# First layer of a four-layer image kernel: its matmuls cut into 32x32 tiles, its weighting by w2 and sum over branches moved to TensorE

## The chip, the cores and the metric

The kernel runs on 1 core of one Trainium2 chip. The metric is the device time of one execution in microseconds (us); lower is better. Five engines work at once, each with its own queue of instructions: TensorE (PE: matmuls, with their weight loads shown apart as PEld), VectorE (DVE), ScalarE (ACT), GpSimd (POOL) and SyncE (SP: it issues the DMAs). They wait for one another by semaphores.

## What is computed

x holds 8 images of 128 x 128 pixels with 32 channels. Four layers follow, each on a normalised x and each added to x. The change touches the first alone:

```python
def _gn(v, G=32, eps=1e-05):          # per image and channel over all pixels
    ...
def _L0_conv_ref(x, w1, wg, w2):      # w1, w2: (32, 4); wg: (4, 32, 32)
    y = _gelu(x[..., :, None] * w1)
    z = _gelu(jnp.einsum('bhwim,moi->bhwmo', y, wg))
    out = jnp.einsum('bhwmc,cm->bhwc', z, w2)
    return out
...
x = x + _L0_conv_ref(_gn(x), L0_conv_w1, L0_conv_wg, L0_conv_w2)
x = x + _L1_conv_ref(_gn(x), L1_conv_kernel)
x = x + _L2_conv_ref(_gn(x), ...)
x = x + _L3_conv_ref(_gn(x), ...)
```

So the first layer has four branches m. In each, every channel is scaled by w1[:, m] and goes through gelu (y), a 32x32 matrix wg[m] mixes the channels, a second gelu gives z, and the output is the sum of w2[:, m] * z over the four branches. All of it is float32.

## The kernel before

The 8 images are worked in two slabs of 4 (s = 0, 1). A slab's 4 images x 32 channels fill the 128 partitions (partition = 32 * image + channel), and its 16,384 pixels lie along the free dimension of the SBUF tile X. A slab goes through 8 stages (0: load and transpose, 1: the first layer, 2: the second, 3 and 4: the third, 5 to 7: the fourth); all engines meet between stages (stage_end). After both slabs comes a last part that scales and stores.

Stage 1 takes the slab in 8 chunks of 2048 pixels (CHUNK), each with 4 branches, so a slab has 32 units k = 4 * i + m. A unit is:

- gelu_y (L547, ACT): y = gelu(scale * X chunk + bias), 128 x 2048, into yb[m]; the normalisation and w1 are folded into scale and bias (l0s).
- the matmuls of L333 (PE): 4 matmuls of 128 x 512 with wg[m], which is stored as a block-diagonal 128 x 128 matrix with wg[m] once per image, into 4 of the 8 PSUM banks. Even branches take banks 0 to 3, odd ones 4 to 7, so PE can project one unit while ACT reads the other.
- gelu_z (L554, ACT): gelu of the 4 banks into zb[m % 2].
- L698 (DVE): acc = zb * w2[:, m] + acc, 128 x 2048; the last of the four writes X.

ACT's order is gelu_y(k + 2), gelu_z(k), gelu_y(k + 3), gelu_z(k + 1) and so on: the y of two units ahead lies between two z. Only at the slab's end are there z with no y between them (the last three). PE's L330 waits for y of unit k (s_y) and for the bank set to be free (s_zs, slot(k): z of unit k - 2 has been read). gelu_z waits for the projection (s_zp) and for a free zb (s_x1). The semaphores made by rsem are rings: slot(k) lets work k start when work k - ring is done, after(k) waits for work k itself. After each chunk DVE measures X with four bn_stats (L704), after the last it aggregates them (L676), POOL works out the next layer's coefficients (L953 to L956), and stage 2 begins.

Stages named below: stage 3 has matmuls 32 columns wide (L410: output partitions C * g, all 128 rows), stage 4 has matmuls of 32 rows by 64 columns (L448, function r_sum: 8 combinations of row group and column half) and transposes (L459); ACT copies the results of L448 (L614). The last part has, again and again, 4 transposes (L515) and a matmul of 512 columns (L253).

Of the kernel before, what the change touches and what calls it, by code (L numbers as in the profile page):

```python
# [24 lines left out]
G = P // C  # L25
# [42 lines left out]
def build(nc, x, consts, choose, out):  # L68
# [5 lines left out]
    with ctx:  # L74
# [19 lines left out]
        bns = sb("bns", 16)  # L94
        ps = ctx.enter_context(nc.psum_tensor("ps", [P, 8, BANK], fp32))
# [10 lines left out]
        wg = c("wg").rearrange("p (m n) -> p m n", m=MULTI)  # L106
        wq = c("wq").rearrange("p (h n) -> p h n", h=HEADS)
# [24 lines left out]
        zb, _e = part(_e, [RING, CHUNK])  # L132
        acc, _ = part(_e, [CHUNK])
# [55 lines left out]
        s_zs = rsem("z_ready", "act")  # L189
        s_x1 = rsem("z_added", "dve")  # L190
# [117 lines left out]
        def _(pe):  # L308
# [3 lines left out]
            for s in range(NS):  # L312
# [14 lines left out]
                with pe.Fori(0, PIX // CHUNK) as i:  # L327
                    for m in range(MULTI):
                        k = s * UNITS + i * MULTI + m
                        pe.wait_ge(s_y, k + 1)  # L330
                        pe.wait_ge(s_zs, slot(k))
                        for b in range(4):
                            last = pe.matmul(ps[:, 4 * (m % 2) + b, :], wg[:, m, :], yb[:, m, b * BANK:(b + 1) * BANK],  # L333
                                             start=True, stop=True)
                        last.then_inc(s_zp, 1)
# [192 lines left out]
        def _(act):  # L528
# [5 lines left out]
            for s in range(NS):  # L534
# [131 lines left out]
        def _(dve):  # L666
            start_rings(dve, "dve")
            for s in range(NS):
# [430 lines left out]
```

## Time and profile before

| | us |
|---|---|
| median of 3 runs | 1118.27 (1116.99 to 1118.3) |
| the profiled execution, its own time | 1117.37 |
| its span, first to last instruction | 1115.4 |
| busy PE / DVE / ACT / POOL | 888.9 / 845.1 / 600.1 / 324.9 |
| stage 1, first slab, first gelu_y to first coefficient | 130.4 (41.09 to 171.51) |
| stage 1, second slab | 129.9 (520.01 to 649.91) |

The time of an execution is 1.97 us over its span. The two runs of stage 1 are 23% of the span. A busy time is the union of an engine's instructions: overlapping ones are counted once, so "busy" is no measure of how much work goes through. The granted clock of PE has two levels, 1.2 GHz (0.50 in the profile) and 2.4 GHz (1.00). Each float32 matmul of the code stands in the trace as two MATMUL records, each with a weight load of its own: the 4 matmuls x 64 units of L333 are 256 in the code and 512 in the trace. The start of a group of instructions, its length, its engine, its line and its tiles are one row of the timeline; "idle before" is how long that engine had stood still and who released it.

### The profile page before, as it was taken

The numbers are of one execution on the slowest core, as the hardware profiler recorded it, in microseconds if no ns is written. First come the engines' busy times: TensorE is split into PE (matmuls) and PEld (weight loads), VectorE is DVE, ScalarE is ACT, GpSimd is POOL, SyncE is SP. The second block draws the span as 40 slices with busy tenths as digits, with TensorE's granted clock in tenths as the row PEclk, the third lists the DMA queues.
The fourth block names the chain that finished last, engine by engine and source line by source line (L and its number), as shares of the span: only waits on it lengthen the run. The fifth ranks groups of instructions, "written<-read, shape, count | busy, mean of one in ns | idle before, by whom it ended". The sixth has DMA issues, their size and how long they took to land. (4 is left out here: it accounts for less than half of the span.)

```text
span 1115.4 us, 21429 instructions
## 1 busy us (share of the span) xinstructions
PE 888.9 (80%) x6876; PEld 591.1 (53%) x6876; DVE 845.1 (76%) x1207; ACT 600.1 (54%) x695; POOL 324.9 (29%) x265
## 2 busy tenths in 40 slices
PE   5699986979997667965999949799966588676774
PEld 4343336978875465343433349788854563233332
DVE  7577787987868844885778879877778446799796
ACT  5899982323333153546999923233332444466564
POOL 0000008500009910510000067000089304465564
PEclk8899997989998678988999969999986688899897
DMA  9100000000000020242000000000000200033334
GB/s 304 36 1 0 0 0 1 0 1 1 0 1 2 1 75 3 72 139 88 0 0 0 0 1 1 1 1 0 1 2 2 75 0 1 0 114 113 113 113 151
DMA packets 51305, 39.40 MB, mean 35 GB/s; under 512 B 1600, under 2 KB 50880, under 8 KB 51008
## 3 DMA queue, kind: packets, MB, share of 16 engines
q1 hardware_dynamic: 51264, 38.85, 11.0%
q8 instruction: 25, 0.41, 0.1%
q14 instruction: 16, 0.13, 0.0%
HBM read 22.07 MB, written 16.78 MB: 35 GB/s over the span
## 5 line engine op out<-in xcount | busy, mean ns | idle before, releaser
L333 PE MATMUL ps<-work,cst 128*128 128x512 f32 x512 | 235.9, 608 | 17.3 <-ACT work L547 13.5
L333 PEld LDWEIGHTS ps<-work,cst 128*128 128x128 f32 x512 | 94.3, 193 | 157.6 <-issue 143.4
L547 ACT ACTIVATE work<-X,l0s 128x2048 f32 (+1 forms) x64 | 136.7, 2141 | 3.8 <-SPq L291 3.8
L253 PE MATMUL ps<-ST,work 128*128 128x512 f32 (+1 forms) x256 | 131.7, 638 | 7.5 <-DVE work L866 5.4
L554 ACT ACTIVATE work<-ps 128x2048 f32<-128x2048 f32 x64 | 123.1, 1924 | 7.1 <-PE ps L333 6.8
L988 POOL TENSOR_TENSOR work<-cst,ksum 128x512 f32<-128x512 f32 x64 | 69.5, 1105 | 174.5 <-SPq L291 172.6
L778 DVE TENSOR_TENSOR work<-ps,cst 64x512 f32<-64x512 f32 x128 | 88.1, 688 | 37.8 <-PE ps L400 36.0
L953 POOL TENSOR_TENSOR co<-mv,cst 128x1 f32<-128x1 f32 x8 | 1.5, 189 | 383.0 <-DVEq L243 296.7
L576 ACT ACTIVATE work<-ps 128x512 f32<-128x512 f32 x80 | 47.8, 597 | 99.6 <-PE ps L353 99.6
L1023 POOL TENSOR_TENSOR work<-X,work 128x512 f32<-128x512 f32 x64 | 82.1, 1286 | 58.9 <-DVE work L913 58.9
L364 PE MATMUL ps<-cst,work 128*128 128x143 f32 x640 | 96.5, 296 | 1.4 <-DVE X L728 1.2
L698 DVE SCALAR_TENSOR_TENSOR work<-work,cst 128x2048 f32<-128x2048 f32 x32 | 75.2, 2351 | 24.5 <-ACT work L554 24.3
L913 DVE SCALAR_TENSOR_TENSOR work<-work 128x512 f32<-128x512 f32 x64 | 92.1, 1444 | 0.0
L364 PEld LDWEIGHTS ps<-cst,work 128*128 128x128 f32 x640 | 86.3, 196 | 5.0 <-DVE X L728 3.3
L640 ACT ACTIVATE work<-work,bns 128x512 f32<-128x512 f32 x64 | 52.0, 813 | 58.7 <-DVE work L908 58.7
L585 ACT ACTIVATE work<-ps 128x512 f32<-128x512 f32 x64 | 38.2, 597 | 83.7 <-PE ps L400 83.7
L476 PE MATMUL ps<-cst,work 128*128 128x96 f32 x512 | 62.2, 288 | 23.1 <-ACT work L623 23.1
L623 ACT ACTIVATE work<-X,co 128x512 f32 x64 | 51.4, 812 | 51.7 <-POOLq L243 44.4
L459 PE MATMUL ps<-cst,work 128*128 128x128 f32 x256 | 52.4, 352 | 32.5 <-DVE X L820 32.4
L1007 POOL TENSOR_TENSOR work<-work 128x512 f32<-128x512 f32 x32 | 40.6, 1270 | 124.4 <-ACT work L635 124.4
L515 PE MATMUL ps<-cst,work 128*128 128x128 f32 x256 | 45.7, 305 | 39.0 <-POOL work L1023 38.8
L515 PEld LDWEIGHTS ps<-cst,work 128*128 128x128 f32 x256 | 29.2, 150 | 87.0 <-POOL work L1023 87.0
(96 smaller groups left out, 1649.3 us busy)
## 6 DMA issues: line engine op xcount, KB each, us to landing
work<-x SPq DMA_DIRECT2D x32, 512.0 KB, 4.6
out<-work SPq DMA_DIRECT2D x64, 256.0 KB, 2.8
work<-choose SPq DMA_DIRECT2D x2, 2048.0 KB, 7.9
cst<-consts SPq DMA_DIRECT2D x1, 1009.5 KB, 9.0
cst<-consts SPq DMA_DIRECT2D x1, 64.0 KB, 1.9
```

The lines of the kernel that those rows point to most:

```text
L253: return nc.tensor.matmul(ps[:, bank, :], sel[:, n, :], ST[:, ds(s * (4 * H), 4 * H)], start=True, stop=True)
L333: last = pe.matmul(ps[:, 4 * (m % 2) + b, :], wg[:, m, :], yb[:, m, b * BANK:(b + 1) * BANK], start=True, stop=True)
L364: last = pe.matmul(ps[:, DEEP + 2 * (q % 2) + par, at:at + OW * OH], patch[:, q, k, :], c("fir"), start=True, stop=True)
L476: last = pe.matmul(ps[:, u, w * COLS:w * COLS + COLS], xc[:, u, w * H:w * H + H], c("w9"), start=True, stop=True)
L515: last = pe.transpose(ps[:, DEEP + n % DEEP, w * P:w * P + P], row[:, n % ROWS, w * H:w * H + H], ident)
L547: act.activation(yb[:, m, :], X[:, ds(s * PIX + i * CHUNK, CHUNK)], ACT.Gelu, scale=l0s[:, m:m + 1], bias=l0s[:, MULTI + m:MULTI + m + 1]) ...
L554: act.activation(zb[:, m % 2, :], ps[:, 4 * (m % 2):4 * (m % 2) + 4, :].rearrange("p a b -> p (a b)"), ACT.Gelu).then_inc(s_zs, 1)
L698: dve.scalar_tensor_tensor(acc if m < MULTI - 1 else x_in, zb[:, m % 2, :], c("w2")[:, m:m + 1], acc if m else x_in, ALU.mult, ALU.add).th ...
L778: last = dve.tensor_tensor(o, k_in, bias, ALU.add)
L913: dve.scalar_tensor_tensor(row[:, u, :], row[:, u, :], LEAKY, row[:, u, :], ALU.mult, ALU.max).then_inc(s_fl, 1)
L988: pool.tensor_tensor(qb[:, hf, :, :, :], c("bq").rearrange("p (j o i) -> p j o i", o=1, i=WS).broadcast_to([P, WS, half, WS]), ksum[:, ds( ...
L1023: pool.tensor_tensor(rows4(row[:, u, :]), columns(s, n), rows4(row[:, u, :]), ALU.add).then_inc(s_fo, 1)
```

## The change

The projection is cut into 16 matmuls per unit. Tile (g, k4) takes image g's 32 partitions of yb (rows 32g to 32g + 31), piece k4 of 512 pixels, and the 32x32 block of wg[m]; it writes to PSUM bank g, partitions 32 * k4 to 32 * k4 + 31. The four banks 0 to 3 then hold z with the pieces along the partitions and the images along the banks. gelu_z reads these four banks in every unit (before: two sets of four in turn), so the projection of unit k + 1 waits for gelu_z(k).

The weighting and sum are 16 more matmuls per unit (weigh_z). Each has 32 rows (piece k4) and 32 columns (image g), its weights are diag[rows, m, :], a 32x32 diagonal matrix of w2[:, m], and it adds to bank 4 + k4, partitions 32g onwards, from the first branch (start) to the last (stop). Banks 4 to 7 so hold the sum over the branches in X's own layout, and DVE adds them to X once per chunk. weigh_z of a chunk's first branch waits until DVE has read the chunk before. zb and acc shrink to zb alone; w2d is a new tile of 128 columns, filled by four POOL instructions at the start.

PE's program for stage 1 is no longer a loop: it is written out for the 32 units, in the order projection of unit k + 1, then weigh_z of unit k.

```diff
-                with pe.Fori(0, PIX // CHUNK) as i:
+                def project_y(i, m):
+
+                    k = s * UNITS + i * MULTI + m
+                    pe.wait_ge(s_y, k + 1)
+                    pe.wait_ge(s_zs, slot(k))
+                    for k4 in range(4):
+                        for g in range(G):
+                            rows = slice(C * g, C * g + C)
+                            last = pe.matmul(ps[C * k4:C * k4 + C, g, :], wg[rows, m, C * g:C * g + C],
+                                             yb[rows, m, k4 * BANK:(k4 + 1) * BANK], start=True, stop=True)
+                    last.then_inc(s_zp, 1)
+
+                def weigh_z(i, m):
+
+                    k = s * UNITS + i * MULTI + m
+                    pe.wait_ge(s_zs, after(k, 1))
+                    if m == 0:
+                        pe.wait_ge(s_x1, slot(i + s * (PIX // CHUNK)))
+                    for g in range(G):
+                        for k4 in range(4):
+                            rows = slice(C * k4, C * k4 + C)
+                            last = pe.matmul(ps[C * g:C * g + C, 4 + k4, :], diag[rows, m, :], zb[rows, m % 2, g, :],
+                                             start=(m == 0), stop=(m == MULTI - 1))
+                    last.then_inc(s_ws, 1)
+
+                pe.wait_ge(s_diag, 1)
+                project_y(0, 0)
+                for i in range(PIX // CHUNK - 1):
                     for m in range(MULTI):
-                        k = s * UNITS + i * MULTI + m
-                        pe.wait_ge(s_y, k + 1)
-                        pe.wait_ge(s_zs, slot(k))
-                        for b in range(4):
-                            last = pe.matmul(ps[:, 4 * (m % 2) + b, :], wg[:, m, :], yb[:, m, b * BANK:(b + 1) * BANK],
-                                             start=True, stop=True)
-                        last.then_inc(s_zp, 1)
+                        project_y(i + (m + 1) // MULTI, (m + 1) % MULTI)
+                        weigh_z(i, m)
...
                 def gelu_z(i, m):
                     k = s * UNITS + i * MULTI + m
                     act.wait_ge(s_zp, k + 1)
-                    act.wait_ge(s_x1, slot(k))
-                    act.activation(zb[:, m % 2, :], ps[:, 4 * (m % 2):4 * (m % 2) + 4, :].rearrange("p a b -> p (a b)"),
-                                   ACT.Gelu).then_inc(s_zs, 1)
+                    act.wait_ge(s_ws, slot(k))
+                    act.activation(zb[:, m % 2, :, :], ps[:, 0:4, :], ACT.Gelu).then_inc(s_zs, 1)
...
                 with dve.Fori(0, PIX // CHUNK) as i:
+                    n = i + s * (PIX // CHUNK)
                     x_in = X[:, ds(s * PIX + i * CHUNK, CHUNK)]
-                    for m in range(MULTI):
-                        k = s * UNITS + i * MULTI + m
-
-                        dve.wait_ge(s_zs, after(k))
-                        dve.wait_ge(s_x1, slot(k) + 1)
-                        dve.scalar_tensor_tensor(acc if m < MULTI - 1 else x_in, zb[:, m % 2, :],
-                                                 c("w2")[:, m:m + 1], acc if m else x_in, ALU.mult, ALU.add
-                                                 ).then_inc(s_x1, 1)
+                    dve.wait_ge(s_ws, after(i * MULTI + (s * UNITS + MULTI - 1)))
+                    dve.scalar_tensor_tensor(x_in, ps[:, 4:8, :].rearrange("p a b -> p (a b)"), 1.0, x_in,
+                                             ALU.mult, ALU.add).then_inc(s_x1, 1)
```

On TensorE, at the start of stage 1, the row of the program before (one loop body, run 8 times; "x4" are four matmuls in a row):

```order
L327 UNCONDITIONAL_BRANCH
L327 ISA
L333 MATMUL ps<-work,cst 128x512 x4
L330 REGISTER_ALU
L333 MATMUL ps<-work,cst 128x512 x4
L330 REGISTER_ALU
L333 MATMUL ps<-work,cst 128x512 x4
```

and of the changed program, where L338 is the projection and L351 the weighting:

```order
L338 MATMUL ps<-work,cst 32x512 x32
L351 MATMUL ps<-work,w2d 32x512 x16
L338 MATMUL ps<-work,cst 32x512 x16
L351 MATMUL ps<-work,w2d 32x512 x16
L338 MATMUL ps<-work,cst 32x512 x16
L351 MATMUL ps<-work,w2d 32x512 x16
```

The first two projections stand together, then weighting and projection take turns, and each projection stands ahead of the weighting of the unit before it.

On VectorE, in the same stage, before:

```order
L697 REGISTER_ALU [waits z_ready]
L698 ISA [waits z_added]
L698 SCALAR_TENSOR_TENSOR work<-work,cst,X 128x2048
L696 REGISTER_ALU
L698 SCALAR_TENSOR_TENSOR work<-work,cst 128x2048 [waits z_added,z_ready]
L696 REGISTER_ALU
L698 SCALAR_TENSOR_TENSOR work<-work,cst 128x2048 [waits z_added,z_ready]
```

and of the changed program:

```order
L719 UNCONDITIONAL_BRANCH [waits stage_ended]
L719 ISA
L723 ISA [waits z_weighted_and_summed]
L723 SCALAR_TENSOR_TENSOR X<-ps,X 128x2048
L725 REGISTER_ALU
L728 ISA [waits chunk_added]
```

Four instructions per chunk have become one, which waits for PE where the four waited for ACT. The order on ScalarE is as it was; gelu_z now waits for z_weighted_and_summed where it waited for z_added.

## Rows read from the trace of the kernel before

**Rows 1.** Steady stage 1: length, busy PE, PEld, DVE, ACT, POOL; PEclk.
```profile
99.39:155.55 56.16, 55.04 (x121) 21.59 (x120) 43.34 (x30) 56.16 (x32) 0.00 (x0) 1.00 0.00 0
```

**Rows 2.** L333: ns min/median/max; L554: busy us, mean ns | idle before, releaser.
```profile
L333 PE MATMUL ps<-work,cst x512: 592/592/1222, 43.2 to 641.1; 128*128 128x512 f32 x171
...
L554 ACT ACTIVATE work<-ps 128x2048 f32<-128x2048 f32 x64 | 123.1, 1924 | 7.1 <-PE ps L333 6.8
```

**Rows 3.** Timeline of the steady part: start us, length us, engine, line.
```profile
101.37 1.93 ACT L554 ACTIVATE work<-ps 128x2048 f32<-128x2048 f32 x1
...
103.42 0.30 PEld L333 LDWEIGHTS ps<-work,cst 128*128 128x128 f32 x2 [0.87 <-issue]
103.95 0.19 PEld L333 LDWEIGHTS ps<-work,cst 128*128 128x128 f32 x1 [0.24 <-issue]
104.38 0.19 PEld L333 LDWEIGHTS ps<-work,cst 128*128 128x128 f32 x1 [0.24 <-issue]
...
105.12 1.93 ACT L554 ACTIVATE work<-ps 128x2048 f32<-128x2048 f32 x1
```

**Rows 4.** Timeline, start of stage 1, first slab, then second.
```profile
41.09 6.06 ACT L547 ACTIVATE work<-X,l0s 128x2048 f32<-128x2048 f32 x3 [1.19 <-SPq L291]
43.24 23.41 PE L333 MATMUL ps<-work,cst 128*128 128x512 f32 x49 [6.75 <-ACT work L547]
48.97 1.88 ACT L554 ACTIVATE work<-ps 128x2048 f32<-128x2048 f32 x1 [1.82 <-PE ps L333]
...
527.37 1.88 ACT L554 ACTIVATE work<-ps 128x2048 f32<-128x2048 f32 x1 [1.29 <-PE ps L333]
```

**Rows 5.** Timeline, end of stage 1, first slab.
```profile
157.51 3.98 ACT L554 ACTIVATE work<-ps 128x2048 f32<-128x2048 f32 x2
...
163.36 1.88 ACT L554 ACTIVATE work<-ps 128x2048 f32<-128x2048 f32 x1 [1.87 <-PE ps L333]
165.27 2.35 DVE L698 SCALAR_TENSOR_TENSOR X<-work,cst 128x2048 f32 x1 [0.93 <-ACT work L554]
```

**Rows 6.** Timeline, groups of small tiles in stages 3 and 4.
```profile
260.02 1.08 PE L410 MATMUL ps<-work 128*32 128x128 f32 x32
...
335.56 1.26 PE L448 MATMUL ps<-work,cst 32*64 32x128 f32 x64 [2.05 <-ACT work L614]
...
336.88 1.94 ACT L614 ACTIVATE work<-ps 128x1024 f32<-128x1024 f32 x2 [1.37 <-PE ps L448]
...
365.84 2.01 PE L448 MATMUL ps<-work,cst 32*64 32x128 f32 x64
```

**Rows 7.** Inside the L448 group at 335.56: weight loads, then matmuls in flight.
```profile
335.56:335.67 0.11, 0.11 (x16) 1.00 0.00 0
...
335.80:335.81 0.01, 0.01 (x16) 1.00 0.00 0
```

**Rows 8.** PE busy, granted clock: last part, stage 4, stage 1's start.
```profile
990.00:1020.00 30.00, 22.31 (x89) 1.00 0.46 140
372.00:390.00 18.00, 10.95 (x101) 0.59 0.00 1
...
47.00:48.00 1.00, 1.00 (x4) 0.85 0.00 0
```

**Rows 9.** Timeline of PE: last part, then stage 4.
```profile
983.39 0.66 PE L515 MATMUL ps<-cst,work 128*128 128x128 f32 x4 [0.56 <-POOL work L1023]
983.88 1.02 PE L253 MATMUL ps<-ST,work 128*128 x2
...
378.91 2.24 PE L459 MATMUL ps<-cst,work 128*128 128x128 f32 x8 [2.03 <-DVE X L820]
```

**Rows 10.** VectorE reading PSUM; the page's instruction fetches; POOL after loading.
```profile
L908 DVE SCALAR_TENSOR_TENSOR work<-X,vall,ps 128x512 f32<-128x512 f32 x64 | 47.1, 735 | 7.7 <-PE ps L253 7.6
...
q8 instruction: 25, 0.41, 0.1%
...
38.86 0.19 POOL L953 TENSOR_TENSOR co<-mv,cst 128x1 f32<-128x1 f32 x1 [25.42 <-DVE mv L676]
```

More of the change, by code:

```diff
@@ L94, in build @@
         bns = sb("bns", 16)
+        w2d = sb("w2d", MULTI * C)
         ps = ctx.enter_context(nc.psum_tensor("ps", [P, 8, BANK], fp32))
@@ L106, in build @@
         wg = c("wg").rearrange("p (m n) -> p m n", m=MULTI)
+        diag = w2d[:, :].rearrange("p (m c) -> p m c", m=MULTI)
         wq = c("wq").rearrange("p (h n) -> p h n", h=HEADS)
@@ L131, in build @@
         yb, _e = part(0, [DEEP, CHUNK])
-        zb, _e = part(_e, [RING, CHUNK])
-        acc, _ = part(_e, [CHUNK])
+        zb, _ = part(_e, [RING, G, BANK])
         strip, _e = part(0, [DEEP, H, PW])
@@ L188, in build @@
         s_zp = sem("z_projected")
-        s_zs = rsem("z_ready", "act")
-        s_x1 = rsem("z_added", "dve")
+        s_diag = sem("w2_diagonals_ready")
+        s_zs = rsem("z_ready", "act", 1)
+        s_ws = rsem("z_weighted_and_summed", "pe")
+        s_x1 = rsem("chunk_added", "dve", 1)
         s_strip = sem("strip_ready")
@@ L324, in _ @@
                 stage_end(pe, s, 0)
-                with pe.Fori(0, PIX // CHUNK) as i:
-                    for m in range(MULTI):
-                        k = s * UNITS + i * MULTI + m
-                        pe.wait_ge(s_y, k + 1)
-                        pe.wait_ge(s_zs, slot(k))
-                        for b in range(4):
-                            last = pe.matmul(ps[:, 4 * (m % 2) + b, :], wg[:, m, :], yb[:, m, b * BANK:(b + 1) * BANK],
-                                             start=True, stop=True)
-                        last.then_inc(s_zp, 1)
+                def project_y(i, m):
[22 more added lines that the diff above has]
+                for i in range(PIX // CHUNK - 1):
+                    for m in range(MULTI):
+                        project_y(i + (m + 1) // MULTI, (m + 1) % MULTI)
+                        weigh_z(i, m)
+                for m in range(MULTI):
+                    if m + 1 < MULTI:
+                        project_y(PIX // CHUNK - 1, m + 1)
+                    weigh_z(PIX // CHUNK - 1, m)
                 stage_end(pe, s, 1)
@@ L691, in _ @@
                 with dve.Fori(0, PIX // CHUNK) as i:
+                    n = i + s * (PIX // CHUNK)
                     x_in = X[:, ds(s * PIX + i * CHUNK, CHUNK)]
-                    for m in range(MULTI):
-                        k = s * UNITS + i * MULTI + m
-                        dve.wait_ge(s_zs, after(k))
-                        dve.wait_ge(s_x1, slot(k) + 1)
-                        dve.scalar_tensor_tensor(acc if m < MULTI - 1 else x_in, zb[:, m % 2, :],
-                                                 c("w2")[:, m:m + 1], acc if m else x_in, ALU.mult, ALU.add
-                                                 ).then_inc(s_x1, 1)
-                    dve.wait_ge(s_x1, after(k))
+                    dve.wait_ge(s_ws, after(i * MULTI + (s * UNITS + MULTI - 1)))
+                    dve.scalar_tensor_tensor(x_in, ps[:, 4:8, :].rearrange("p a b -> p (a b)"), 1.0, x_in,
+                                             ALU.mult, ALU.add).then_inc(s_x1, 1)
+                    dve.wait_ge(s_x1, after(n, 1))
                     alone(dve)
@@ L932, in _ @@
             pool.wait_ge(s_const, 16)
+            for m in range(MULTI):
+                last = pool.tensor_scalar(diag[:, m, :], c("mean8")[:, 0:C], c("w2")[:, m:m + 1], float(B),
+                                          ALU.mult, ALU.mult)
+            last.then_inc(s_diag, 1)
             pool.tensor_tensor(c("wk"), c("wk"), c("temp"), ALU.mult)
```

## The prediction

> **What bounds the kernel now.** I read the steady part of stage 1 first, by engine [rows 1]. ScalarE is busy for the whole of its 56.16 us, VectorE for 43.34; TensorE shows 55.04, but a busy TensorE may be waiting inside its group, so that alone does not decide. The timeline does [rows 3]: gelu_z starts at 101.37 and at 105.12 with one gelu_y between them and no idle time before either; the steady stretch is 15 units from y to y, so a unit takes 56.16 / 15 = 3.74 us. ScalarE is the bound, with one z and one y per unit. The next view is who released ScalarE [rows 2]: over both slabs gelu_z waited 7.1 us in all, 6.8 of them for the matmuls. The timeline puts them at the two ends of each slab: 1.82 us before the first z of slab one, 1.29 in slab two [rows 4], 1.87 before the last z of slab one [rows 5], which leaves 1.8 for that of slab two. So of some 260 us in stage 1 only 6.8 can be won on ScalarE without making its own instructions faster, and the change leaves these as they are: the same 128 x 2048 from the same kind of operands. What VectorE loses, three of four 2.35 us passes per chunk, is work beside a bound engine.
>
> The question is then whether TensorE's new work stays hidden behind ScalarE, and what it does at the slab's ends.
>
> **How long a projection group takes (A).** Before, a weight load comes every 0.43 us (103.95, 104.38) [rows 3], and a matmul record of 512 columns lasts 592 ns at the 2.4 GHz level [rows 2]. So 0.427 us of it is streaming and 0.165 the way through. A unit's 8 records took 3.42 + 0.17 = 3.6 us. Now there are 16 tiles with 2 records each. No row has 16 tiles, but two kinds come near [rows 6]. L410 puts 32 records on 4 column tiles, so 8 records of 128 columns (a quarter, 0.107 us) per tile: 0.854 us if the tiles run side by side; it takes 1.08. L448 puts 64 records on 8 tiles (4 row groups, 2 column halves), again 8 per tile and 0.854 us; it takes 1.26. If tiles stood in line, they would take 3.4 and 6.8 us. Small tiles do run together. The two passes of one matmul don't hold up the next tile either: inside the L448 group 16 weight loads are under way 0.11 us after its start, and by 335.80 there are 16 matmuls in flight [rows 7].
>
> A tile of the changed kernel streams 2 x 0.427 = 0.854 us, the same. The start is new: 32 weight loads at 16 per 0.11 us are spread over 0.22 us. A = 0.22 + 0.854 + 0.165 = 1.24 us. Bounds: 1.08 as L410, and, if all that L448 takes over its streaming (0.41) doubles with twice the tiles, 0.854 + 0.82 = 1.67. I take 1.24, which lies by the L448 row of 1.26. At 1.2 GHz L448 takes 2.01 [rows 6], and A would be about 2.05.
>
> By the span rule of the Trainium skill (TensorE: Matmul & The Clock Gate, section "Measured speedup vs the span model") 16 tiles cost one matmul plus 4 ns for each further tile. As an estimate by it, with two passes, A would be 592 + 427 + 15 x 4 ns = 1.08 us and the whole about 1.0 us faster than with 1.24, 1119.9 us; the row of L410 agrees with that size, that of L448 is above it.
>
> **The steady part.** The projection of k + 1 now waits for gelu_z(k), because there is one set of banks. z starts at 0, ends after 1.93 (up to 1.99 late in a slab: the 3.98 us for two near its end [rows 5]); TensorE begins 0.12 later (103.30 to 103.42 [rows 3]), and ScalarE starts 0.05 after a tiled group ends (335.56 + 1.26 = 336.82 to 336.88 [rows 6]). With the next z due at 3.74, a projection is hidden up to A = 3.74 - 1.96 - 0.12 - 0.05 = 1.61 us. At 1.24 there are 0.37 us of cover. Each 0.1 us over 1.61 would cost 0.1 x some 60 units = 6 us; this is the cover that matters. The weighting follows the projection on the same queue: some 1.24 more, together 2.5 of 3.74 us, so TensorE then stands still for 1.2 us until the next projection may start. It is needed two units later (slot(k) of a ring of two). At a chunk's start it waits for VectorE: after the last z of a chunk ends, weighting is done at 0.12 + 1.24 + 1.05 = 2.4 us, the addition of 2.35 us at 4.8; TensorE comes to that wait at about 4.1, stands 0.8 us with nothing behind it but a projection whose z ends at 7.5, and costs nothing. VectorE, with 43.34 of 56.16 us before [rows 1], loses three passes of 2.35 us in each 15 us and is far from a bound. The addition reads PSUM now; L908, which does, takes 735 ns for 512 [rows 10], so 2.35 at the least and 2.94 for four times that at the most; on the path once per slab: 0 to 0.6, I take 0.05, since the fixed part is paid once. The steady part changes by 0.
>
> **The head of a slab.** The three y of 41.09 end after 6.06 us, at 47.15; the first z started 1.82 us later, since 8 full records began at 43.24 with the clock at 1.2 GHz, and the clock rose only between 47 and 48 [rows 4, 8]. A cold A of 2.05 ends at 45.3. Saved: the 1.82 us, and 1.29 in the second slab. But TensorE then stands still until 49, so the clock is low for the next one or two projections: each is 2.05 - 1.61 = 0.44 us over the cover. I take 0.6 per slab (bounds 0 and 1.3). Head: -1.2 and -0.7.
>
> **The tail of a slab.** The last two z have no y between them, so A lies bare. Count from the start of the z at 157.51. Before: VectorE's last pass starts at 165.27, 7.76 us later [rows 5]. Now: z ends 1.99, TensorE + 0.12 + A, z + 0.05 + 1.88, again 0.12 + A + 0.05 + 1.88, then the last weighting 0.12 + A, and VectorE 0.05 behind: 6.26 + 3A. With A = 1.24 that is 9.98, and 0.05 for PSUM: + 2.27 us per slab. The weighting, which was VectorE's own pass, is a step more at the end. With A = 1.08 the tail is + 1.8, with 1.67 + 3.6.
>
> **What is left.** POOL's four small instructions lie in its 25.42 us of waiting [rows 10]: 0. The loop written out makes TensorE's code for stage 1 eight times as many matmul groups, each fetched once, where the page has 25 fetches in all [rows 10]. The L448 groups are written out too, and 64 records ran through without a hole [rows 6], so I take 0. As an upper bound I let every second group grow by all that L448 has over its streaming, 0.41: 0.04 over the cover, 31 times, + 1.2 us. Later stages are unchanged.
>
> **Sum.** Tail 2 x 2.27 = + 4.5, head - 1.9, the rest 0: + 2.6 us. From the profiled execution, 1117.37 (span 1115.4 and 1.97 around it), that is 1120.0; the median of the runs is 0.9 higher, so 1120.9 us. What a measurement can tell from no change is about 0.2%, 2.2 us: the forecast lies on that edge.
>
> **The rivals.** (1) The clock flickers. TensorE now stands still for 1.2 us in each unit; before it was busy for 55.04 of 56.16 us. For it: at the end of stage 4, with TensorE busy 10.95 of 18 us and gaps of 2.03 us, the mean granted clock was 0.59 [rows 8, 9]. Against: the last part has 1.52 us of matmuls and 0.56 of standing still in turn, is busy 22.31 of 30 us, and kept 1.00 throughout. The new stage 1 is busy 2.5 of 3.74 us, 67%, between 61% and 74%. And a slow clock makes it busy nearly always (2.05 + 2.05 of 4.2 us), as when it rose at 47 us. So it would come and go: each unit at 1.2 GHz costs 0.44 us, a third of 62 units 9 us, all of them 27. I price it at + 9: 1130. The Trainium skill has it as a rule (same page, section "A second HAM failure mode: psum-queue depth-cycling"): short idle times between groups of matmuls that go round PSUM banks make the clock swing.
>
> (2) Sixteen tiles don't run together, only eight: each half streams 0.854, A = 0.22 + 1.71 + 0.165 = 2.09, 0.48 over the cover for 62 units = 30, tail + 5: about 1156 us. For it: nothing in the trace has 16 tiles. Against: per partition L410 reads four streams from SBUF at once and L448 writes four banks at once, the same as here, each at nearly full speed. It decides from A = 1.61 on.
>
> (3) Faster: the head's gain of 3.1 us stays whole (the clock rises at once), and the tail costs less. With 6.26 + 3A - 7.76 the tail cannot fall under + 1.1 for A = 0.854, bare streaming, so - 3.1 + 2.2 = - 0.9 us is the best by this account: 1117.4. To be over 0.2% faster, ScalarE's cadence itself must shorten, by 0.04 us of 3.74 in 62 units, if VectorE's passes over zb and acc had slowed it. Against: with no engine beside them three y take 6.06, 2.02 each, and a z 1.88 [rows 4]; in the steady part a y and a z together take 3.74, no more than the two alone. It would give 1115.
>
> **Chances.** Forecast (cadence kept, ends cost 0 to 4.5 us) 0.60, of which 0.29 lies over + 2.2 us and 0.31 within; clock flickers 0.15, of which 0.02 within; half concurrency, or A over the cover in another way, 0.14, of which all slower; faster by a shorter cadence or something else 0.11, of which 0.09 over 0.2% and 0.02 within. So faster 0.09, same 0.35, slower 0.56. The predicted time is the forecast's. The range from 1115 to 1134 holds the forecast, the faster case and most of the flickering clock; it leaves out the half concurrency and a clock that is low most of the time.
>
> **What would show it.** In the profile after: z every 3.74 us in the steady part, with no idle time before it; a projection group of 32 records with 1.1 to 1.6 us (over 1.61 refutes the cover, and ScalarE's idle time before gelu_z then names TensorE); the first z near 47.1; the last z and VectorE's last pass with 1.8 to 2.7 us more between the third last z and that pass; the granted clock at 1.00 from about 54 us to the end of stage 1. Stages 2 to 7 should keep their lengths. If the time is far over 1134, look at A; if it is under 1115, at the distance between two gelu.

## The result, and the profile after

The changed kernel takes 1108.37 us (median of 4 runs, 1106.56 to 1109.82) against 1118.04 us (1116.99 to 1118.3) for the kernel before on the same chip: ratio 0.9914, 95% interval 0.9897 to 0.9932. The forecast was 1120.9 us, with a range of 1115 to 1134: the time is outside it, on the faster side.

The profiled execution took 1109.82 us, its span is 1108.0. The head of the page of the changed kernel: busy time, share and instructions of each engine.

```profile
span 1108.0 us, 28376 instructions
PE 805.2 (73%) x10460; PEld 545.8 (49%) x10460; DVE 724.1 (65%) x1159; ACT 600.6 (54%) x695; POOL 337.9 (31%) x269
```

ScalarE is as before (600.1 us), and VectorE has lost 121 us of work. Neither tells where 7.4 us of span went. I cut both traces at VectorE's bn_aggregate of each stage and compared the pieces (from each mark to the next, in us):

| | before | after | difference |
|---|---|---|---|
| up to the first layer, slab one | 37.76 | 39.22 | +1.46 |
| first layer, slab one / two | 132.65 / 132.13 | 133.91 / 133.56 | +1.26 / +1.43 |
| second layer, slab one / two | 72.38 / 72.47 | 72.13 / 71.49 | -0.25 / -0.98 |
| third and fourth, both slabs, and loading of slab two | 513.61 | 513.06 | -0.55 |
| last part, to the end | 154.42 | 144.64 | **-9.78** |

The first piece was between 37.8 and 39.8 us in all profiled kernels, so its 1.46 says nothing of the change. The first layer, which the change rewrites, became slower, and by about what the forecast says; nearly half of that comes back in the second layer. The whole gain is in the last part, where the change alters no instruction.

**What the last part does.** It handles 64 banks of 512 pixels. For each, VectorE's scaled pass (L908, after L932) reads PSUM, its leaky pass (L913, after L937; a leaky rectifier, the larger of a value and a fraction of it) reads and writes SBUF, and GpSimd adds the result to X (L1023, after L1051; below this is "the addition"). GpSimd's loop over the banks has eight of them in its body; "an eight" below is one turn of it. These are the groups of both passes over SBUF in the page of the kernel before: busy us, mean ns of one | idle time before them and its releaser.

```profile
L1023 POOL TENSOR_TENSOR work<-X,work 128x512 f32<-128x512 f32 x64 | 82.1, 1286 | 58.9 <-DVE work L913 58.9
L913 DVE SCALAR_TENSOR_TENSOR work<-work 128x512 f32<-128x512 f32 x64 | 92.1, 1444 | 0.0
```

and in that of the changed kernel:

```profile
L1051 POOL TENSOR_TENSOR work<-X,work 128x512 f32<-128x512 f32 x64 | 93.7, 1482 | 37.6 <-DVE work L937 37.6
L937 DVE SCALAR_TENSOR_TENSOR work<-work 128x512 f32<-128x512 f32 x64 | 82.7, 1296 | 0.0
```

The addition became slower and idles less, and the leaky pass became faster. The timeline of VectorE and GpSimd before shows the rhythm (start us, length us, engine, line):

```profile
970.74 0.69 DVE L913 SCALAR_TENSOR_TENSOR work<-work 128x512 f32<-128x512 f32 x1
...
975.86 1.27 POOL L1023 TENSOR_TENSOR work<-X,work 128x512 f32<-128x512 f32 x1 [0.80 <-DVE work L913]
976.19 1.49 DVE L913 SCALAR_TENSOR_TENSOR work<-work 128x512 f32<-128x512 f32 x1
977.60 0.73 DVE L908 SCALAR_TENSOR_TENSOR work<-X,vall,ps 128x512 f32<-128x512 f32 x1
977.93 1.26 POOL L1023 TENSOR_TENSOR work<-X,work 128x512 f32<-128x512 f32 x1 [0.80 <-DVE work L913]
978.26 1.48 DVE L913 SCALAR_TENSOR_TENSOR work<-work 128x512 f32<-128x512 f32 x1
```

A leaky pass with no addition beside it takes 0.69 us (970.74). The one at 976.19 starts 0.33 us behind the addition and takes 1.49: the addition ends at 977.13, and the pass 0.55 us later, at 977.68, as if it had stood still until then. Only 0.25 later, at 977.93, the next addition starts. The cycle is 1.27 + 0.55 + 0.25 = 2.07 us per bank. The same stretch of the changed kernel:

```profile
976.07 1.27 POOL L1051 TENSOR_TENSOR work<-X,work 128x512 f32<-128x512 f32 x1 [0.81 <-DVE work L937]
976.39 1.49 DVE L937 SCALAR_TENSOR_TENSOR work<-work 128x512 f32<-128x512 f32 x1
977.81 0.73 DVE L932 SCALAR_TENSOR_TENSOR work<-X,vall,ps 128x512 f32<-128x512 f32 x1
978.45 5.18 POOL L1051 TENSOR_TENSOR work<-X,work 128x512 f32<-128x512 f32 x3 [1.11 <-DVE work L937]
978.47 0.68 DVE L937 SCALAR_TENSOR_TENSOR work<-work 128x512 f32<-128x512 f32 x1
979.73 1.09 DVE L937 SCALAR_TENSOR_TENSOR work<-work 128x512 f32<-128x512 f32 x1
981.40 1.10 DVE L937 SCALAR_TENSOR_TENSOR work<-work 128x512 f32<-128x512 f32 x1
```

The third addition comes 0.31 late (1.11 idle, not 0.80). Now the leaky pass takes 0.68, and the addition is the one held up (three take 5.18). By the records the addition even starts 0.02 us ahead of the pass (978.45 against 978.47) and loses all the same; in the five traces that switch in this way the lead is 0.005 to 0.02 us. From here on GpSimd is one bank behind and never waits for a semaphore. The cycle is 1.68 us: an addition of 1.27 and some 0.41 in which the leaky pass has its turn. The 0.25 us from the leaky pass's end to the next addition has left the path. Slab one stays so to its end, slab two does not, as GpSimd's busy time shows; two stretches of 30 us, one in each slab, of the kernel before:

```profile
980.00:1010.00 30.00, 18.76 (x15) 1.00 0.41 125
1062.00:1092.00 30.00, 18.79 (x15) 1.00 0.46 140
```

and of the changed kernel:

```profile
980.00:1010.00 30.00, 30.00 (x19) 1.00 0.46 141
1062.00:1092.00 30.00, 18.03 (x15) 1.00 0.46 138
```

From first to last addition slab one took 63.07 us before and 53.20 after, slab two 63.05 and 63.43. That is 9.5 of the 9.8 us.

VectorE's scaled pass, which reads PSUM beside an addition in the second rhythm, stays at 0.73. The Trainium skill (SBUF — State Buffer, section "SBUF: two separate sides") describes this: a VectorE operation with two SBUF inputs and a GpSimd operation that reads SBUF share one pair of ports as a lock, held for the whole instruction by whoever starts first. The rows agree, 0.69 alone and 1.49 behind an addition, except that the recorded starts don't say to the last 0.02 us who is first.

**Why the third addition is late.** Of the changed kernel's edits only one touches GpSimd's own program: the four instructions that fill w2d, run at about 13.4 us. GpSimd's records around this place, register steps included (operation, start us, line; before, then after):

```
FUSED_REGOPS  977.71 L1023        FUSED_REGOPS  977.92 L1051
TENSOR_TENSOR 977.93 L1023        ALU_OP        978.43 L1050
ALU_OP        978.22 L1022        TENSOR_TENSOR 978.45 L1051
```

Elsewhere ALU_OP starts 0.2 us behind FUSED_REGOPS and the addition 0.02 behind ALU_OP. Both kernels have one pause of some 0.3 us: from FUSED_REGOPS to ALU_OP are 0.51 us at this place. Before, it falls behind the start of the fourth addition, under its 1.26 us, and costs nothing. After, it falls ahead of the third addition. The pause comes back at the same instruction in each of the seven later eights, but shorter: 0.28 us from FUSED_REGOPS to ALU_OP in both kernels, 0.09 more than elsewhere. So it belongs to a place in the code. It also explains slab two of the changed kernel: there each third addition of an eight comes only 0.09 late, and the rhythm stays:

```profile
1037.58 1.27 POOL L1051 TENSOR_TENSOR work<-X,work 128x512 f32<-128x512 f32 x1 [0.81 <-DVE work L937]
1039.73 1.27 POOL L1051 TENSOR_TENSOR work<-X,work 128x512 f32<-128x512 f32 x1 [0.89 <-DVE work L937]
1041.81 1.26 POOL L1051 TENSOR_TENSOR work<-X,work 128x512 f32<-128x512 f32 x1 [0.80 <-DVE work L937]
```

My theory: the pause sits at a fixed place of GpSimd's program, and longer code ahead of it moves other instructions to that place. The rival: VectorE's, ScalarE's or TensorE's new work in the first layer moves something that decides how the last part begins.

### The profile page after: what moved, and what is told of

It is laid out like the page before. It is cut to its first block and busy times, and to the rows that moved or that the text cites. A ratio compares the mean times of both kernels' runs of the same rounds, so it can differ in the third digit from the quotient of the medians.

```text
span 1108.0 us, 28376 instructions
## 1 busy us (share of the span) xinstructions
PE 805.2 (73%) x10460; PEld 545.8 (49%) x10460; DVE 724.1 (65%) x1159; ACT 600.6 (54%) x695; POOL 337.9 (31%) x269
## 5 line engine op out<-in xcount | busy, mean ns | idle before, releaser
L723 DVE SCALAR_TENSOR_TENSOR X<-ps,X 128x2048 f32 x16 | 36.7, 2292 | 185.1 <-PE ps L351 185.1
L338 PE MATMUL ps<-work,cst 32*32 32x512 f32 x2048 | 78.2, 633 | 101.8 <-ACT work L583 88.0
L1051 POOL TENSOR_TENSOR work<-X,work 128x512 f32<-128x512 f32 x64 | 93.7, 1482 | 37.6 <-DVE work L937 37.6
L338 PEld LDWEIGHTS ps<-work,cst 32*32 32x32 f32 x2048 | 17.9, 105 | 160.0 <-issue 159.9
L351 PE MATMUL ps<-work,w2d 32*32 32x512 f32 x2048 | 91.4, 612 | 2.3 <-ACT work L583 1.8
L393 PEld LDWEIGHTS ps<-cst,work 128*128 128x128 f32 x640 | 85.5, 195 | 4.8 <-DVE X L752 3.2
L937 DVE SCALAR_TENSOR_TENSOR work<-work 128x512 f32<-128x512 f32 x64 | 82.7, 1296 | 0.0
L488 PE MATMUL ps<-cst,work 128*128 128x128 f32 x256 | 51.7, 350 | 34.2 <-DVE X L844 34.1
L505 PEld LDWEIGHTS ps<-cst,work 128*128 128x128 f32 x512 | 61.3, 203 | 24.3 <-ACT work L651 24.3
```

The source lines that it names most:

```text
L338: last = pe.matmul(ps[C * k4:C * k4 + C, g, :], wg[rows, m, C * g:C * g + C], yb[rows, m, k4 * BANK:(k4 + 1) * BANK], start=True, stop=True)
L351: last = pe.matmul(ps[C * g:C * g + C, 4 + k4, :], diag[rows, m, :], zb[rows, m % 2, g, :], start=(m == 0), stop=(m == MULTI - 1))
L393: last = pe.matmul(ps[:, DEEP + 2 * (q % 2) + par, at:at + OW * OH], patch[:, q, k, :], c("fir"), start=True, stop=True)
L505: last = pe.matmul(ps[:, u, w * COLS:w * COLS + COLS], xc[:, u, w * H:w * H + H], c("w9"), start=True, stop=True)
L937: dve.scalar_tensor_tensor(row[:, u, :], row[:, u, :], LEAKY, row[:, u, :], ALU.mult, ALU.max).then_inc(s_fl, 1)
L1051: pool.tensor_tensor(rows4(row[:, u, :]), columns(s, n), rows4(row[:, u, :]), ALU.add).then_inc(s_fo, 1)
```

## The experiments

### The four GpSimd instructions alone, then two, then one

The kernel before, with the instructions that fill w2d, its tile and its semaphore; nothing reads it.

```diff
             pool.wait_ge(s_const, 16)
 
+            for m in range(MULTI):      # range(2), range(1) in the next two
+                last = pool.tensor_scalar(w2d[:, m * C:m * C + C], c("mean8")[:, 0:C], c("w2")[:, m:m + 1], float(B),
+                                          ALU.mult, ALU.mult)
+            last.then_inc(s_diag, 1)
```

> The kernel before with one thing of the change alone: the four small GpSimd instructions at the start that fill w2d, which nothing reads. Theory S (a stall of GpSimd's own instruction stream, whose place shifts by four instructions, lands before the third output addition of slab one and sets a faster rhythm there): the additions of slab one start every 1.68 us where they started every 2.07, 30 of them, so 11 to 12 us faster than before, about 1106.5 us. Theory T (TensorE's or VectorE's lighter first layer, or the shifted start of the last part, sets the rhythm): the same as before, 1118 us, both slabs at 2.07.

Measured: 1107.39 us (1105.95 to 1118.8) against 1117.58, ratio 0.9918 (0.9895 to 0.9942). The four instructions alone bring all of the gain; the rival is out. Of ten executions one took 1118.8, as would one in which the switch didn't come; it has no trace, so that stays a guess. None of the 25 executions of the kernel before beside these runs was under 1115.84.

> The kernel before with two of the four small GpSimd instructions at the start. Theory S: the stall now lies between two instructions of GpSimd while it waits for VectorE anyway, so nothing follows: 1118 us, both slabs at 2.07 us per addition. A theory in which the extra instructions matter as work or as writes to SBUF gives a part of the gain, 1106 to 1114 us. Theory T: 1118 us.

Measured: 1117.8 us, ratio 0.9997 (0.9988 to 1.0007). Both slabs keep 2.07. This kernel has the same new tile and semaphore as the one with four, so neither of them makes the gain.

> The kernel before with one small GpSimd instruction at the start. Theory S: the stall lies between the register step and the fourth addition of slab one, so that addition comes some 0.3 us late and the faster rhythm of 1.68 us begins one addition later than with four instructions: about 1107 us. A theory in which the amount of extra work matters: between 1114 and 1118 us. Theory T: 1118 us.

Measured: 1107.18 us, ratio 0.9903 (0.9881 to 0.9924). One instruction does what four do, one addition later: the distances between its additions are 2.07, 2.38, 1.78, 1.68. So it is not the amount of work. GpSimd's program has three instructions per addition, so a shift by four is one whole addition and one instruction, a shift by one that instruction alone: both put the pause ahead of an addition, a shift by two or zero does not.

### The changed kernel without instructions added to GpSimd

```diff
# VectorE, after moments(NB) of stage 0
+                if s == 0:
+                    dve.wait_ge(s_const, 16)
+                    for m in range(MULTI):
+                        last = dve.tensor_scalar(diag[:, m, :], c("mean8")[:, 0:C], c("w2")[:, m:m + 1], float(B),
+                                                 ALU.mult, ALU.mult)
+                    last.then_inc(s_diag, 1)
# GpSimd: the same four instructions are gone
```

> The changed kernel with the four instructions that fill w2d on VectorE, behind the first slab's moments, where GpSimd works out coefficients meanwhile; GpSimd's program is then as long as before. Theory S: the last part falls back to 2.07 us per addition in both slabs and the time is what the first layer alone makes of it, about 1120 to 1121 us. Theory T: 1108 us as the changed kernel.

Measured: 1117.67 us, ratio 1.0001 (0.9991 to 1.0011). With everything of the change but the shift, the gain is gone. It is also some 2.5 us under the 1120 to 1121 expected: by the whole time the new first layer cost nothing that can be told from the spread. The timeline of its last part has the old rhythm:

```profile
978.42 1.26 POOL L1053 TENSOR_TENSOR work<-X,work 128x512 f32<-128x512 f32 x1 [0.80 <-DVE work L943]
978.75 1.48 DVE L943 SCALAR_TENSOR_TENSOR work<-work 128x512 f32<-128x512 f32 x1
```

### GpSimd held one bank back, in both kernels

If the rhythm is a matter of who starts first, one wait sets it: the first addition of each eight waits until the leaky pass of the bank after it is done too.

```diff
-                        pool.wait_ge(s_fl, s * NB + i * ROWS + (u + 1))
+                        pool.wait_ge(s_fl, s * NB + i * ROWS + (2 if u == 0 else u + 1))
```

> The kernel before, with one wait changed: GpSimd's first output addition of every eight waits for VectorE's second leaky pass instead of its first, so GpSimd is one bank behind. Theory S with a rhythm of two states (GpSimd one bank behind works without a pause beside VectorE at 1.68 us per bank; GpSimd that has caught up starts ahead of VectorE's pass, holds it up and then waits itself, 2.07): both slabs at 1.68, 2 x 30 x 0.39 = 23 us less, about 1095 us. If the faster rhythm needed the stall itself or the changed first layer: 1118 us, or a little more for the added wait.

Measured: 1099.48 us (1097.27 to 1100.33) against 1117.07, ratio 0.9837 (0.9819 to 0.9856). Both slabs run at 1.68, with 2.54 and 1.23 at the start of each eight, where the wait costs; that, six times 0.41 us, is part of why it is 4 us over the 1095 expected. The groups of its page:

```profile
L1023 POOL TENSOR_TENSOR work<-X,work 128x512 f32<-128x512 f32 x64 | 103.2, 1647 | 19.2 <-DVE work L913 19.2
L913 DVE SCALAR_TENSOR_TENSOR work<-work 128x512 f32<-128x512 f32 x64 | 74.2, 1164 | 0.0
```

The same edit in the changed kernel:

> The changed kernel with the same wait changed in the last part. Theory S: slab two gains 11 to 12 us as well, about 1096 us; against the kernel before with the same wait it shows the first layer's change by itself, 0 to 2.6 us slower (2.6 was forecast; where the last part was alike, the comparison so far gave 0.1). If the gain of the changed kernel was another one than the rhythm, it would stay some 10 us ahead of the kernel before with the wait: 1085 us.

Measured: 1098.41 us (1098.24 to 1100.0), ratio 0.9834 (0.9818 to 0.9851). With the rhythm fixed in both, the two kernels are 1.1 us apart, the changed one ahead, within the spread of either. Its first layer takes 133.56 us in each slab against 132.34 and 132.13, its second layer 71.20 and 71.26 against 72.26 and 72.41: for both layers and both slabs 0.4 us more.

### A delay of GpSimd at one place

Small additions on GpSimd ahead of the output addition, in one bank of eight (u == 3), in the kernel before: one, three, then five. Each of the three was executed once.

```diff
                         pool.wait_ge(s_fl, s * NB + i * ROWS + (u + 1))
+                        if u == 3:
+                            for q in range(5):      # range(1), range(3), other columns of l0s
+                                pool.tensor_tensor(l0s[:, 3 + q:4 + q], c("gamma"), c("beta"), ALU.add)
```

> The kernel before with one addition of 128x1 on GpSimd ahead of its output addition of every fourth bank in eight; nothing reads its result. It delays that addition by 0.14 to 0.19 us. In the slow rhythm GpSimd starts 0.33 us ahead of VectorE's pass, so it would still be ahead: slab two stays at 2.07 us per bank. In slab one the fixed place of the stall now falls between the register step and the fourth output addition, so it switches to 1.68 after the fourth: about 1107 us. If any delay, however short, switches the rhythm: both slabs at 1.68, 1096 us.

Measured: 1106.72 us. Slab one switches, slab two does not (one distance of 2.16 in each eight, and the kernel with one GpSimd instruction at the start has 2.15 there with no small addition): one small addition hardly delays anything by itself, but moves the code.

> The same with three such additions: 0.4 to 0.5 us, more than the 0.33 us by which GpSimd is ahead. Theory of the two-state rhythm: both slabs switch to 1.68 us per bank at the fourth bank, about 1097 us with the small work added. If the rhythm hung on the place of the code alone, slab two would stay at 2.07: 1107 or 1118 us.

Measured: 1120.45 us: the expectation failed. Three small additions, pipelined, take 0.49 us in all and delay the output addition by 0.26 (2.33 between additions, not 2.07). The timeline shows that this was just too little:

```profile
994.92 0.49 POOL L1025 TENSOR_TENSOR l0s<-cst 128x1 f32<-128x1 f32 x3 [0.63 <-DVE work L913]
995.35 1.27 POOL L1026 TENSOR_TENSOR work<-X,work 128x512 f32<-128x512 f32 x1
995.42 1.75 DVE L913 SCALAR_TENSOR_TENSOR work<-work 128x512 f32<-128x512 f32 x1
```

The addition is still 0.07 ahead, so the leaky pass is held for longer than ever, 1.75 us, and nothing switches; both slabs keep 2.07 elsewhere. In this kernel no pause falls ahead of an addition. I had taken the size of the delay from the number of instructions. The one with five:

> As e7_late3, with five small GpSimd additions ahead of every fourth bank in eight. In e7_late3 three of them still let the output addition start 0.07 us ahead of VectorE's pass (995.35 against 995.42), and the rhythm stayed at 2.07 us. Two more of 0.14 us each put it 0.2 us behind that pass. Theory of order (who starts first holds the other up): both slabs switch to 1.68 us per bank, 56 banks x 0.39 less 8 x 0.3 for the added work, 1098 to 1102 us. If only the place of the code counts: 1107 us or more, slab two at 2.07.

Measured: 1104.42 us, slower than the 1098 to 1102 expected. The switch comes in both slabs at the fourth bank:

```profile
1042.68 1.23 POOL L1025 TENSOR_TENSOR l0s<-cst 128x1 f32<-128x1 f32 x5 [0.63 <-DVE work L913]
1043.19 0.68 DVE L913 SCALAR_TENSOR_TENSOR work<-work 128x512 f32<-128x512 f32 x1
```

The leaky pass is ahead by now and takes 0.68. The rest to the time expected is the price of the delay itself, 0.71 us in each later eight (2.85 and 1.22, where two banks take 3.36), where 0.3 was taken. So the rhythm has a threshold between the delays tried: 0.26 us leaves it, 0.31 (the 2.38 of the changed kernel) and 1.01 (the 3.08 of this one) turn it. In the lead of the addition over the leaky pass that is 0.07 us against 0.02 and less. That is also why a pause of 0.3 us decides over 10.

### The first layer's own rhythm, with a shorter y

Both kernels show the same cadence in the first layer because ScalarE bounds it. To see what TensorE would allow, y was cut to 512 of its 2048 columns. Both kernels leave out three quarters of y's work, so they don't compute the layer and only show times; each was executed once.

```diff
-                    act.activation(yb[:, m, :], X[:, ds(s * PIX + i * CHUNK, CHUNK)], ACT.Gelu,
+                    act.activation(yb[:, m, 0:BANK], X[:, ds(s * PIX + i * CHUNK, BANK)], ACT.Gelu,
...
+                for m in range(MULTI):      # once per slab, so that all of yb is written
+                    act.activation(yb[:, m, :], X[:, ds(s * PIX, CHUNK)], ACT.Gelu, ...)
+                act.drain()
```

> The kernel before with gelu_y on 512 of 2048 columns (the rest of yb keeps values written once ahead of the stage), so ScalarE has some 2.4 us per unit where it had 3.74. It shows what binds the first layer once ScalarE doesn't. Before, TensorE has 8 records of 0.427 us and a gap, so a unit should take 3.5 to 3.7 us: next to nothing gained in 64 units (5 to 15 us).

Measured: 1116.35 us against 1118.69; z every 3.43 us, each waiting for TensorE:

```profile
102.05 1.88 ACT L554 ACTIVATE work<-ps 128x2048 f32<-128x2048 f32 x1 [0.86 <-PE ps L333]
105.48 1.88 ACT L554 ACTIVATE work<-ps 128x2048 f32<-128x2048 f32 x1 [0.86 <-PE ps L333]
```

3.43 is 8 records of 0.427: the term of 0.427 us per record holds, and the old projection had 0.31 of 3.74 us to spare. The total fell by 2.3 us only, not 5 to 15: the four full gelu at each slab's head take 8.05 us, and the first z then waits 5.19 us, which eats most of what the shorter y gives.

> The changed kernel with the same short gelu_y. With one set of banks z and projection follow one another: 1.9 + 0.12 + 1.15 + 0.05 = 3.25 us per unit, 0.5 us less than ScalarE's 3.74, so some 30 us under the changed kernel, about 1078 us. If TensorE's 16 tiles were the bound instead (projection and weighting in turn, 2.5 us), a unit would take 2.5 to 2.7 us: 70 us under, about 1040 us.

Measured: 1099.72 us; z every 3.34 us:

```profile
104.42 1.88 ACT L583 ACTIVATE work<-ps 128x2048 f32<-128x2048 f32 x1 [0.85 <-PE ps L338]
106.44 1.15 PE L338 MATMUL ps<-work,cst 32*32 32x512 f32 x32 [1.00 <-ACT work L583]
107.76 1.88 ACT L583 ACTIVATE work<-ps 128x2048 f32<-128x2048 f32 x1 [0.76 <-PE ps L338]
```

From one z to the next: z 1.88, TensorE + 0.14, projection 1.15, and + 0.17 to the next z, 3.34, near the 3.25 expected. The expected total of 1078 was far off: I had forgotten the four full gelu at each slab's head, some 8 us per slab (16 of the 22 us that are missing), and 3.34 in place of 3.25 is some 5.6 us more; the first layer took 128.25 and 128.03 us. The changed kernel's chain is z, projection, z, and is only 0.4 us under the cadence of 3.74: a faster y would shorten that cadence by 11%.

### Held back once per slab

The hold at each eight costs 0.41 us every time (2.54 + 1.23 against 3.36), and after the switch the rhythm holds itself. So the kernel before, with the hold on the first addition of each slab alone:

```diff
-                with pool.Fori(0, NB // ROWS) as i:
...
+                for u in range(ROWS):
+                    output(0, u, 2 if u == 0 else 1)
+                with pool.Fori(1, NB // ROWS) as i:
                     for u in range(ROWS):
...
+                        output(i, u, 1)
# output(i, u, ahead): wait_ge(s_fl, s * NB + i * ROWS + (u + ahead)), then the addition
```

> The kernel before, where GpSimd waits for VectorE's second leaky pass once per slab only, not in every eighth bank (the first eight banks are written out of the loop for that). In e3_hold_before each later hold cost 2.54 + 1.23 - 2 x 1.68 = 0.41 us, six times. If the lag of one bank keeps itself: no holds later, every bank 1.68, 2.5 us under e3_hold_before, about 1096.5 us. If the lag is lost in time without the hold: some banks at 2.07 and a time between 1099 and 1117 us.

Measured: 1096.61 us (1096.34 to 1096.88) against 1117.49, ratio 0.9813 (0.9797 to 0.9830). It beats both kernels. GpSimd in the same two stretches as above (the second reaches to within 3 us of the end of the span, 1095.1):

```profile
980.00:1010.00 30.00, 30.00 (x19) 1.00 0.49 149
1062.00:1092.00 30.00, 25.28 (x16) 0.89 0.51 155
```

and its groups:

```profile
L1021 POOL TENSOR_TENSOR work<-X,work 128x512 f32<-128x512 f32 x64 | 105.6, 1687 | 14.9 <-DVE work L913 14.9
L913 DVE SCALAR_TENSOR_TENSOR work<-work 128x512 f32<-128x512 f32 x64 | 71.6, 1123 | 0.0
```

From first to last addition a slab takes 51.6 us, both times (before 63.1 and 63.0). This edit with the changed first layer was not run; by the runs with the hold at each eight I estimate a difference of a microsecond or so.

## Why the prediction was wrong, step by step

**A, the length of a projection group: right, a little long.** The timeline of the changed kernel in the steady part:

```profile
101.74 1.92 ACT L583 ACTIVATE work<-ps 128x2048 f32<-128x2048 f32 x1
103.50 2.14 ACT L576 ACTIVATE work<-X,l0s 128x2048 f32 x1
103.80 1.15 PE L338 MATMUL ps<-work,cst 32*32 32x512 f32 x32 [1.41 <-ACT work L583]
104.66 1.48 PE L351 MATMUL ps<-work,w2d 32*32 32x512 f32 x32
105.48 1.92 ACT L583 ACTIVATE work<-ps 128x2048 f32<-128x2048 f32 x1
```

16 tiles of two records take 1.15 us; 1.24 was forecast, between the 1.08 and 1.26 of [rows 6]. At 1.2 GHz it took 2.02 (2.05 forecast). The two-pass estimate by the Trainium skill's span rule (TensorE: Matmul & The Clock Gate, "Measured speedup vs the span model") was 1.08; the trace lies between it and mine. Rival 2, half concurrency, is out.

**The cadence kept: right.** z at 101.74 and 105.48, 3.74 apart as in [rows 3], with no idle time before it. The projection ends at 104.95, 0.53 us ahead of the z that needs it. Busy time of PE, PEld, DVE, ACT and POOL, then the granted clock, against [rows 1]:

```profile
98.00:158.00 60.00, 37.34 (x1054) 12.56 (x1024) 19.10 (x21) 60.00 (x34) 0.00 (x0) 1.00 0.01 2
```

ScalarE is busy throughout. TensorE is busy 62% of the time, stands still for 1.41 us in each unit, and keeps a clock of 1.00: rival 1 is out. What the Trainium skill tells of another kernel, that short idle times between groups of matmuls made the clock swing (TensorE: Matmul & The Clock Gate, section "A second HAM failure mode: psum-queue depth-cycling"), did not show here. The term of 0 for the loop written out held too: the page of the changed kernel has 57 instruction packets on the queue q8, where [rows 10] has 25, and no z of the steady part waits.

**The head: mechanism right.** ScalarE's timeline at the start of slab one, against [rows 4]:

```profile
42.56 6.06 ACT L576 ACTIVATE work<-X,l0s 128x2048 f32<-128x2048 f32 x3 [1.20 <-SPq L294]
48.53 1.85 ACT L583 ACTIVATE work<-ps 128x2048 f32<-128x2048 f32 x1
...
52.72 1.88 ACT L583 ACTIVATE work<-ps 128x2048 f32<-128x2048 f32 x1 [0.34 <-PE ps L338]
...
56.82 1.88 ACT L583 ACTIVATE work<-ps 128x2048 f32<-128x2048 f32 x1 [0.24 <-PE ps L338]
```

The 1.82 us before the first z are gone, and two later z wait 0.34 and 0.24 at the low clock: 0.58 where 0.6 was taken. In slab two one z waits, 0.34. The clock rose later than "about 54 us", in a stage that began 1.5 us later: it was 0.50 from 43 to 56 us and 1.00 from 57.

**The tail: right.** The timeline of slab one's end, against [rows 5]:

```profile
157.87 1.99 ACT L583 ACTIVATE work<-ps 128x2048 f32<-128x2048 f32 x1
161.32 1.88 ACT L583 ACTIVATE work<-ps 128x2048 f32<-128x2048 f32 x1 [1.46 <-PE ps L338]
164.66 1.88 ACT L583 ACTIVATE work<-ps 128x2048 f32<-128x2048 f32 x1 [1.46 <-PE ps L338]
166.59 1.15 PE L351 MATMUL ps<-work,w2d 32*32 32x512 f32 x32 [0.91 <-ACT work L583]
168.04 2.29 DVE L723 SCALAR_TENSOR_TENSOR X<-ps,X 128x2048 f32 x1 [8.02 <-PE ps L351]
```

From the z at 157.87 to VectorE's addition are 10.17 us; forecast 9.98, before 7.76. The smaller A is given back by ScalarE and VectorE starting later after what releases them (0.16 us from a projection's end to each of the last two z and 0.30 from the weighting's end to VectorE, where 0.05 was taken). VectorE's read of PSUM took 2.29, not 2.40. In this pair of traces the first layer cost +1.26 and +1.43 us, 2.7 where 2.6 was forecast. That it agrees to 0.1 us is in part luck, as the last point of this section shows.

**"Later stages are unchanged": wrong, the step that failed.** With it, **"POOL's four small instructions lie in its 25.42 us of waiting: 0"**. They run at 13.4 us, ahead of that wait, which takes up their 1.4 us; as work they cost nothing. They were priced as work only, and not as a shift of the instructions behind them; that shift changed the last part, a later stage, by -9.8 us. The last part stood in the trace at 983 us [rows 9] but I read it for TensorE's clock alone. Its rows [rows 8, 9] show TensorE waiting 0.56 us for GpSimd; the next step would have shown GpSimd idle for 58.9 us before L1023, behind a leaky pass of twice its own length. That would have named a part worth a rival, though not that a second rhythm 10 us per slab faster exists. No rival stood there; "something else" had 0.11 with the shorter cadence. Without the shift the kernel took 1117.67 us, inside the range, 3.2 under the forecast; it is 0.1 us over the kernel before, where 2.6 was forecast.

**A second, smaller miss: the + 2.6 us.** The second layer gave back 0.25 and 0.98 us. Its first matmuls run at the low clock (four of L353 take 1.06 us at 181.62 before, 0.60 at 184.11), and that stretch is not of constant length. But this also came in the kernel before with four GpSimd instructions, whose first layer took 133.39 us (its first z waited 2.51 us, where [rows 4] have 1.82) and whose second took 71.09. So a microsecond moves between the two stages with the time at which the clock rises, and neither stage alone is a measure of the change. Both stages together take 204.5 to 205.3 us per slab in the nine traces with the old first layer and 204.8 to 206.0 in the three with the new one (those with the short y left out). The means are 0.45 us per slab apart, so the change cost some 0.9 us of the 2.6 forecast. Tail and head are as forecast in themselves; where the rest comes back beyond these stages' spread is not shown.

## What to carry to other kernels

Where GpSimd and VectorE take turns over SBUF, look at which of them is ahead, in the timeline and by the idle time of the one that waits: the same instructions had two stable rhythms here, 2.07 and 1.68 us per bank, and one wait at the start chose the faster and was worth 21 us. Price an instruction added to an engine also as a shift of all that engine's later code, and when a change moves the time, cut both traces into stages before explaining it: the gain may stand 900 us behind the edit. To judge such a change, compare the kernels with the rhythm fixed in both; this change of the first layer was then worth about nothing (1098.4 against 1099.5 us).

## What the hardware showed that I had not expected

- A pause of 0.3 us in GpSimd's own instructions, at a place that follows its code: ahead of the third output addition with four instructions more, ahead of the fourth with one, harmless with none or two; 0.09 us at the same place in each later eight. It looks like a fetch of instructions. The count of packets on the queue q8 does not follow it (25 before and with two, 26 with one or four, but also 26 in the kernel before with a short y, which did not switch). The page has a second instruction queue, q14, and there the trace's packets do: one of 8 KB starts at 978.91 in the kernel before and at 979.11 in the changed one, 0.7 us after the pause ends (978.22 and 978.43), and within 1 us after it in all ten traces where the pause can be seen. That it comes after the pause leaves open which of them makes the other, so the cause stays open.
- Which engine is ahead at the start of an addition decides the rhythm within a few hundredths of a microsecond: a lag of 0.26 us left it, 0.31 turned it, and it then held for all of the 27 or more banks of the slab that followed.
- 16 tiles of 32x32 and 512 columns, float32, ran in 1.15 us at 2.4 GHz, where the same 4 x 128 x 512 of output took some 3.6 us in 128x128 form before (8 records 0.427 us apart, 0.592 long). That is the TensorE side alone; ScalarE bounds the layer in both.
